# Expert numbers for TensorE: one load per routed job, or one load for four inside a gate_up group

## The chip, the cores and the metric

The kernel runs on one core of one Trainium2 chip. The metric is the device time of that core in microseconds (us), as the median of several runs. Three runs of the kernel before gave 379.7, 380.57 and 380.77 us.

## What is computed

The reference is one layer on 2048 tokens of 512 numbers: a cross attention and then a feed-forward part with experts. Cut to the second part, where the change lies:

```python
shared = silu(x @ shared_gate_w) * (x @ shared_up_w) @ shared_down_w
logits = x @ router_w                                  # 8 experts
top_val, top_idx = top_k(logits, 2)
probs[t, top_idx] = sigmoid(top_val)
xin = probs.T[:, :, None] * x[None]
gate, up = split(einsum('etd,edf->etf', xin, gate_up_w), 2)
out = x_in + shared + einsum('eti,eid->etd', silu(gate) * up, down_w).sum(0)
```

Here x is the layer-normed result of the attention part. D is 512, the inner width I is 256, and each token goes to two of the eight experts.

## The kernel before, in words

The work is written by hand as one instruction stream for each engine, tied together with semaphores. The first 16 tiles of 128 tokens run attention and, two tiles later, the shared expert as "jobs" 0 to 15. Then the router's choices are turned into tables. The token choices are sorted by expert and packed into 39 routed jobs of 128 rows, so `TILES` is 16, `ROUTED` 39 and `JOBS` 55. Each routed job has one expert, and its number (1 to 8) stands in the int32 tile `jexpert`, which VectorE writes once (L784). This text counts the routed jobs from 0 to 38.

Matmul operands are split in a high part (`x_hi`, `gu_hi`, `dn_hi`, 32-bit) and a low part. In one routed job the engines do this:

- GpSimd gathers 128 rows of normed x into `xg` by an indirect DMA (L406), four jobs ahead in a ring of four, and adds the result `y` to the output by an indirect DMA (L425). Both go through GpSimd's one queue, in the order gather of job n+4, scatter of job n. Ahead of a scatter the queue waits for `y` and for scatters of earlier jobs (for the first seven jobs: for all of the last three).
- TensorE transposes `xg` (`x_transpose`, L1021), multiplies by the expert's gate_up weights in `gate_up_high` (L909, four matmuls) and `gate_up_low` (L914 and L917, four each), transposes `h` (`h_transpose`, L926), and multiplies by the down weights in `down` (L936, L939, L942, two each).
- ScalarE computes `silu` from the finished gate_up bank (L574 loads the expert number, L575 is the activation), copies the transposed x to `x_hi` and `x_bf` (L490, L491) and the transposed h to `h_hi` and `h_bf` (L498, L499).
- VectorE computes h (L825 loads the expert number, L826), `x_lo` (L648), `h_lo` (L654) and the copy of y (L835).

TensorE's order in iteration n is fixed by the loop at the end of `_(pe)`: load the expert number of job n (L1028), wait for `x_hi` of job n (with others, L903 to L907), `gate_up_high(n)`, `h_transpose(n - 1)`, `gate_up_low(n)`, `x_transpose(n + 1)`, `down(n - 1)`. The four matmuls of L917 wait for `x_lo` of the job (L915), and the last one signals `g_ps`, on which ScalarE's `silu(n)` waits. The number `e` enters the addresses of the weights `gu_hi[:, e, k, :]` and so on, which TensorE's sequencer works out in small register instructions ahead of the matmuls.

[...] The first four jobs load a second number (`jlow`, L1030). The sequencer handles its instructions in order. [...]

Of the kernel before, what the change touches and what calls it, by code (L numbers as in the profile page):

```python
# [8 lines left out]
TILES = T // P  # L9
RT = S // P  # L10
KC = D // P
E, K, I = 8, 2, 256
# [3 lines left out]
ROUTED = (K * T + E * (P - 1)) // P  # L16
JOBS = TILES + ROUTED
# [17 lines left out]
def build(nc, x, ctx, mask, kpad, wq, bq, wk, bk, router_w, gate_up_w, down_w, sg_w, su_w, sd_w, out):  # L35
# [10 lines left out]
    with stack:  # L46
# [12 lines left out]
        def new(name, shape, dt=f32):  # L59
            offset = top_of[0]  # L60
            top_of[0] = (offset + int(np.prod(shape[1:])) * size[dt] + 31) // 32 * 32
            assert top_of[0] <= nc.sbuf_usable_end
            return at(offset, name, shape, dt)
# [81 lines left out]
        jexpert = new("jexpert", [P, ROUTED], i32)  # L145
# [47 lines left out]
        def ps_g(n):  # L193
            return bank[0] if n >= TILES and n % 2 else bank[4]
# [655 lines left out]
        def _(pe):  # L850
# [51 lines left out]
            def gate_up_high(n, e):  # L902
                pe.wait_ge(xhi_s, n + 1)  # L903
                if n > TILES + 1:
                    pe.wait_ge(h_s, n - 1)
                elif n:
                    pe.wait_ge(h_s, min(n, TILES))  # L907
                for k in range(KC):
                    tn.matmul(ps_g(n)[:], x_hi[:, n % TS, k, :], gu_hi[:, e, k, :], start=(k == 0), stop=False)  # L909

            def gate_up_low(n, e):
                pe.wait_ge(xbf_s, n + 1)
                for k in range(KC):
                    tn.matmul(ps_g(n)[:], x_bf[:, n % TS, k, :], gu_lo[:, e, k, :], start=False, stop=False)  # L914
                pe.wait_ge(xlo_s, n + 1)  # L915
                for k in range(KC):
                    last = tn.matmul(ps_g(n)[:], x_lo[:, n % TS, k, :], gu_hi[:, e, k, :], start=False, stop=(k == KC - 1))  # L917
                last.then_inc(g_ps, 1)

            def h_transpose(n):  # L920
                pe.wait_ge(h_s, n + 1)
                if n:
                    pe.wait_ge(hlo_s, n)
                    pe.wait_ge(hbf_s, n)
                for c in range(IC):
                    last = tn.transpose(ps_hT[:, c * P:(c + 1) * P], h[:, n % 2, c * P:(c + 1) * P], ident[:])  # L926
                last.then_inc(hT_ps, 1)

            def down(n, e):
                pe.wait_ge(hhi_s, n + 1)  # L930
                if n > TILES + 1:
                    pe.wait_ge(y_s, n - 1)
                elif n:
                    pe.wait_ge(y_s, min(n, TILES))
                for c in range(IC):
                    tn.matmul(ps_y(n)[:], h_hi[:, n % 2, c, :], dn_hi[:, e, c, :], start=(c == 0), stop=False)  # L936
                pe.wait_ge(hbf_s, n + 1)
                for c in range(IC):
                    tn.matmul(ps_y(n)[:], h_bf[:, n % 2, c, :], dn_lo[:, e, c, :], start=False, stop=False)  # L939
                pe.wait_ge(hlo_s, n + 1)  # L940
                for c in range(IC):
                    last = tn.matmul(ps_y(n)[:], h_lo[:, n % 2, c, :], dn_hi[:, e, c, :], start=False, stop=(c == IC - 1))  # L942
                last.then_inc(y_ps, 1)
# [28 lines left out]
            for s in range(TILES):  # L972
                j = s - LAG
                if s + 1 < B:
                    projections(s + 1)
                if s + 2 < B:
                    ctx_transpose(s + 2)
                if j == 0:
                    pe.wait_ge(lo_s, 3)
                if j >= 0:  # L980
                    gate_up_high(j, SHARED)
                    gate_up_low(j, SHARED)
                if j >= 1:
                    down(j - 1, SHARED)
                if s >= 1:
                    xn_transpose(s - 1)
                if s + 1 < TILES:
                    scores(s + 1)
                if j >= 0:
                    h_transpose(j)  # L990
                    logits(j)

            gate_up_high(TILES - 2, SHARED)
            gate_up_low(TILES - 2, SHARED)
            xn_transpose(TILES - 1)
            logits(TILES - 2)
            down(TILES - 3, SHARED)
            h_transpose(TILES - 2)
            logits(TILES - 1)
            gate_up_high(TILES - 1, SHARED)  # L1000
            gate_up_low(TILES - 1, SHARED)
            pe.wait_ge(pexp_s, TILES)
            ranks()
# [8 lines left out]
            def x_transpose(n):  # L1012
                pe.wait_ge(gt_xg[n % XS], 16 * ((n - TILES) // XS + 1))
                if n > TILES + 1:
                    pe.wait_ge(xbf_s, n - 1)
                    pe.wait_ge(xlo_s, n - 1)
                elif n == TILES:
                    pe.wait_ge(xbf_s, TILES)
                    pe.wait_ge(xlo_s, TILES)
                for k in range(KC):  # L1020
                    last = tn.transpose(ps_xT[n % 2][:, k * P:(k + 1) * P], xg[:, n % XS, k * P:(k + 1) * P], ident[:])  # L1021
                last.then_inc(xT_ps, 1)

            pe.wait_ge(expert_s, 1)
            x_transpose(TILES)
            before = None
            for n in range(TILES, JOBS):
                e = pe.value_load(jexpert[0:1, n - TILES:n - TILES + 1], min_val=0, max_val=E)  # L1028
                if n < TILES + XS:
                    low = pe.value_load(jlow[0:1, n - TILES:n - TILES + 1], min_val=6, max_val=CHUNKS)  # L1030
                    pe.wait_ge(lo_s, low)
                else:
                    pe.wait_ge(lo_s, CHUNKS)
                gate_up_high(n, e)
                if n > TILES:
                    h_transpose(n - 1)
                gate_up_low(n, e)
                if n + 1 < JOBS:
                    x_transpose(n + 1)
                if n > TILES:  # L1040
                    down(n - 1, before)
                before = e
# [24 lines left out]
```

## Time and profile before

| | |
|---|---|
| median of 3 runs | 380.57 us (379.7 to 380.77) |
| the profiled execution | 381.52 us |
| span of its trace | 379.8 us |
| mean granted TensorE clock in it | 0.945 of full speed |
| TensorE busy (matmul) | 331.9 us, 87% |
| VectorE, ScalarE, GpSimd busy | 209.4, 178.4 and 209.3 us |
| the routed jobs' first and last matmul group (L909) | 169.4 and 363.9 us |

Busy time counts matmuls and data instructions. The sequencer's own instructions (register work, loads of a register, waits) are not in it. They can be asked for by line, and then stand under a name that ends in q: PEldq is TensorE's sequencer, ACTq ScalarE's, DVEq VectorE's. [...]

### The profile page before, as it was taken

To read this page: it belongs to the slowest core of one execution; us is meant where nothing else is said; L and a number is where in the kernel's file an instruction comes from. 1 tells how busy PE (TensorE), PEld (TensorE's weight loads), DVE (VectorE), ACT (ScalarE), POOL (GpSimd) and SP (SyncE) were. 2 spreads that over 40 slices of the span, in tenths; PEclk is the share of its full clock that TensorE was granted. 3 is DMA by queue.
4 is the path that set the end of the run, shared out by engine and by line. 5 is a ranking of instruction groups with operands and counts; after the bars stand their busy time and mean duration, and the time that the engine had idled before them with its cause. 6 is when DMAs were issued, how large, how long until landed. Compare 5 with 4: busy or idle time off the path is not lost.

```text
span 379.8 us, 6456 instructions
## 1 busy us (share of the span) xinstructions
PE 331.9 (87%) x1601; PEld 218.8 (58%) x1627; DVE 209.4 (55%) x476; ACT 178.4 (47%) x401; POOL 209.3 (55%) x196
## 2 busy tenths in 40 slices
PE   2868999999999883258999999999999999999981
PEld 1335675667667552235666666666666666666650
DVE  1755888889988469951444334444343344444331
ACT  2467687577675433512443433344434433344430
POOL 0679999877756124075254465555555455555433
PEclk9978899999999898558999999999999999999997
DMA  7856687665563405150344566656655475665635
GB/s 191 301 177 221 183 270 235 211 212 205 176 214 110 168 4 172 25 169 6 78 76 94 83 118 115 135 98 113 103 106 103 99 117 108 113 112 90 108 40 73
DMA packets 29763, 50.61 MB, mean 133 GB/s; under 512 B 5472, under 2 KB 9312, under 8 KB 29728
## 3 DMA queue, kind: packets, MB, share of 16 engines
q0 software_dynamic: 9008, 21.66, 31.6%
q1 hardware_dynamic: 19232, 27.99, 23.1%
q10 hardware_dynamic: 1488, 0.54, 0.7%
q8 instruction: 16, 0.26, 0.3%
q14 instruction: 19, 0.16, 0.1%
HBM read 30.45 MB, written 19.73 MB: 132 GB/s over the span
## 4 chain that ended last, share of the span: by engine, by line
PE 46%; POOL 15%; issue 13%; DMA 8%; DVE 8%; ACT 7%; ACTq 1%; POOLq 0%; DVEq 0%
PE bank L909 11%; PE bank L917 8%; PE bank L914 8%; POOL gu_lo L348 5%; DMA out_rows<-y,jscatter 5%; PE bank L936 4%; PE bank L942 4%; PE bank L939 4%; PE bank L1021 4%; POOL rstd L325 3%; POOL dn_lo L348 3%; PE bank L926 2%; POOL pen L343 2%; ACT bank L472 2%; DMA kpad_in<-in_mask_BxS_bf 2%
## 5 line engine op out<-in xcount | busy, mean ns | idle before, releaser
L425 POOL DMA_INDIRECT out_rows<-y,jscatter x39 | 61.9, 1587 | 87.5 <-DMA out_rows<-y,jscatter 60.1
L826 DVE SCALAR_TENSOR_TENSOR h<-bank,xg,h 128x256 f32<-128x256 f32 x39 | 18.9, 484 | 106.1 <-ACT h L575 93.4
L917 PE MATMUL bank<-gu_hi,x_lo 128*128 (+1 forms) x220 | 71.5, 447 | 0.0
L909 PE MATMUL bank<-gu_hi,x_hi 128*128 (+1 forms) x220 | 67.4, 429 | 3.4 <-issue 3.1
L406 POOL DMA_INDIRECT xg<-xn_rows,jgather x39 | 41.5, 1063 | 29.0 <-DVE jgather L796 14.3
L914 PE MATMUL bank<-gu_lo,x_bf 128*128 (+1 forms) x200 | 55.7, 393 | 1.3 <-issue 0.2
L348 POOL TENSOR_TENSOR gu_lo<-stage,gu_hi 128x1024 bf16<-128x1024 f32 x18 | 42.6, 2372 | 23.6 <-ACT gu_hi L477 23.5
L575 ACT ACTIVATE h<-bank,xg 128x256 f32<-128x256 f32 x39 | 18.5, 474 | 74.5 <-PE bank L917 66.3
L909 PEld LDWEIGHTS bank<-gu_hi,x_hi 128*128 128x128 f32 x220 | 39.1, 193 | 24.9 <-issue 19.5
L917 PEld LDWEIGHTS bank<-gu_hi,x_lo 128*128 128x128 f32 x220 | 42.6, 194 | 13.4 <-issue 0.8
L942 PE MATMUL bank<-dn_hi,h_lo 128*128 (+1 forms) x110 | 46.0, 499 | 0.0
L498 ACT CAST h_hi<-bank 128x256 fp32r<-128x256 f32 x55 | 20.6, 374 | 51.9 <-PE bank L926 50.2
L648 DVE TENSOR_TENSOR x_lo<-bank,x_hi 128x512 fp32r<-128x512 f32 x55 | 37.3, 679 | 5.9 <-ACT x_bf L491 5.7
L936 PE MATMUL bank<-dn_hi,h_hi 128*128 (+1 forms) x110 | 38.9, 435 | 1.6 <-DVE x L668 1.0
L490 ACT CAST x_hi<-bank 128x512 fp32r<-128x512 f32 x55 | 32.0, 581 | 5.2 <-PE bank L1021 4.2
L939 PE MATMUL bank<-dn_lo,h_bf 128*128 (+1 forms) x104 | 32.7, 392 | 0.6 <-issue 0.2
L491 ACT CAST x_bf<-bank 128x512 bf16<-128x512 f32 x55 | 32.9, 598 | 0.0
L914 PEld LDWEIGHTS bank<-gu_lo,x_bf 128*128 128x128 bf16 x220 | 20.6, 100 | 19.7 <-issue 7.0
L654 DVE TENSOR_TENSOR h_lo<-bank,h_hi 128x256 fp32r<-128x256 f32 x55 | 23.1, 420 | 13.8 <-ACT h_bf L499 13.4
L926 PE MATMUL bank<-ident,h 128*128 128x128 f32 x110 | 21.8, 280 | 7.3 <-DVE h L662 6.2
L835 DVE COPY y<-bank 128x512 f32<-128x512 f32 x39 | 26.6, 682 | 1.1 <-PE bank L942 1.1
L926 PEld LDWEIGHTS bank<-ident,h 128*128 128x128 f32 x110 | 14.2, 141 | 22.6 <-DVE h L662 14.5
(125 smaller groups left out, 489.8 us busy)
## 6 DMA issues: line engine op xcount, KB each, us to landing
stage<-in_L_ffn_gate_up_w SPq DMA_DIRECT2D x16, 512.0 KB, 3.7
xin<-in_x SPq DMA_DIRECT2D x16, 256.0 KB, 4.5
xn_rows<-xn SPq DMA_DIRECT2D x16, 256.0 KB, 4.1
stage<-in_L_ffn_down_w SPq DMA_DIRECT2D x8, 512.0 KB, 3.9
out_rows<-x SPq DMA_DIRECT2D x16, 256.0 KB, 4.3
out_rows<-zeros POOLq DMA_DIRECT2D x1, 1024.0 KB, 5.0
ctx_in<-in_ctx SPq DMA_DIRECT2D x1, 768.0 KB, 8.7
xg<-xn_rows,jgather POOLq DMA_INDIRECT x39
```

Source lines behind the costliest of these rows:

```text
L348: g.tensor_tensor(third((gu_lo, dn_lo), c), stage[:, c % 3], third((gu_hi, dn_hi), c).bitcast(f32), ALU.subtract).then_inc(lo_s, 1)
L406: g.indirect_dma_start(out=xg[:, r, :], out_offset=None, in_=xn_dram, in_offset=bass.IndirectOffsetOnAxis(ap=jgather[:, n - TILES:n - TILE ...
L425: g.indirect_dma_start(out=out, out_offset=bass.IndirectOffsetOnAxis(ap=jscatter[:, n - TILES:n - TILES + 1], axis=0), in_=y[:, r, :], in_ ...
L491: a.copy(x_bf[:, n % TS], rows_T(n)).then_inc(xbf_s, 1)
L648: v.tensor_tensor(x_lo[:, n % TS], rows_T(n), x_hi[:, n % TS].bitcast(f32), ALU.subtract).then_inc(xlo_s, 1)
L909: tn.matmul(ps_g(n)[:], x_hi[:, n % TS, k, :], gu_hi[:, e, k, :], start=(k == 0), stop=False)
L914: tn.matmul(ps_g(n)[:], x_bf[:, n % TS, k, :], gu_lo[:, e, k, :], start=False, stop=False)
L917: last = tn.matmul(ps_g(n)[:], x_lo[:, n % TS, k, :], gu_hi[:, e, k, :], start=False, stop=(k == KC - 1))
L926: last = tn.transpose(ps_hT[:, c * P:(c + 1) * P], h[:, n % 2, c * P:(c + 1) * P], ident[:])
L936: tn.matmul(ps_y(n)[:], h_hi[:, n % 2, c, :], dn_hi[:, e, c, :], start=(c == 0), stop=False)
L939: tn.matmul(ps_y(n)[:], h_bf[:, n % 2, c, :], dn_lo[:, e, c, :], start=False, stop=False)
L942: last = tn.matmul(ps_y(n)[:], h_lo[:, n % 2, c, :], dn_hi[:, e, c, :], start=False, stop=(c == IC - 1))
```

## The change

One load for four jobs takes the place of a load at the head of each job. The first load (jobs 0 to 3) moves ahead of the transpose of the first routed job. The loads for jobs 4 to 7, 8 to 11 and so on up to 36 to 38 stand inside `gate_up_low` of jobs 3, 7, ..., 35, between the third and the fourth matmul of L917. Each load is one call over four neighbouring elements of `jexpert` (three in the last), with the same bounds for each value as before. Loads of `jlow` and the loads on ScalarE and VectorE stay.

```diff
+            experts = []
+
+            def load_experts(quad):
+                experts.extend(nc.values_load_multi_w_load_instructions(
+                    jexpert[0:1, 4 * quad:min(4 * quad + 4, ROUTED)], engines=[mybir.EngineType.PE], min_val=0, max_val=E)[1])
+
-            def gate_up_low(n, e):
+            def gate_up_low(n, e, quad=None):
...
                     last = tn.matmul(ps_g(n)[:], x_lo[:, n % TS, k, :], gu_hi[:, e, k, :], start=False, stop=(k == KC - 1))
+                    if k == 2 and quad is not None:
+                        load_experts(quad)
                 last.then_inc(g_ps, 1)
...
             pe.wait_ge(expert_s, 1)
+            load_experts(0)
             x_transpose(TILES)
             before = None
             for n in range(TILES, JOBS):
-                e = pe.value_load(jexpert[0:1, n - TILES:n - TILES + 1], min_val=0, max_val=E)
+                e = experts[n - TILES]
...
-                gate_up_low(n, e)
+                following = (n - TILES + 1) // 4
+                gate_up_low(n, e, following if (n - TILES) % 4 == 3 and n + 1 < JOBS else None)
```

## Rows read from the trace of the kernel before

**Rows 1.** The page: busy time by engine, and the granted clock in 40 slices.
```profile
PE 331.9 (87%) x1601; PEld 218.8 (58%) x1627; DVE 209.4 (55%) x476; ACT 178.4 (47%) x401; POOL 209.3 (55%) x196
...
PEclk9978899999999898558999999999999999999997
```

**Rows 2.** Timeline of TensorE's weight loads, two routed jobs: start, length, engine, line, operation, count.
```profile
248.19 0.76 PEld L909 LDWEIGHTS bank<-gu_hi,x_hi 128*128 128x128 f32 x4 [0.43 <-issue]
...
253.21 0.76 PEld L909 LDWEIGHTS bank<-gu_hi,x_hi 128*128 128x128 f32 x4 [0.43 <-issue]
```

**Rows 3.** Timeline of all engines, 250.8 to 253.6 us: from one job's gate_up to the next.
```profile
250.53 0.86 PE L917 MATMUL bank<-gu_hi,x_lo 128*128 x3
250.76 0.19 PEld L917 LDWEIGHTS bank<-gu_hi,x_lo 128*128 128x128 f32 x1
...
252.06 0.48 ACT L575 ACTIVATE h<-bank,xg 128x256 f32<-128x256 f32 x1 [1.78 <-PE bank L917]
...
252.43 0.58 ACT L490 CAST x_hi<-bank 128x512 fp32r<-128x512 f32 x1
```

**Rows 4.** L1028 and L905 on TensorE's sequencer, all jobs, then L905 in 250.5 to 253.6: min/median/max ns, first and last start.
```profile
L1028 PEldq TENSOR_LOAD <-jexpert x39: 296/302/948, 166.4 to 361.5; - x39
L1028 PEldq FUSED_REGOPS  x39: 151/151/165, 167.2 to 361.8; - x39
L1028 PEldq SEQ_ASSERT  x39: 18/18/32, 167.4 to 362.0; - x39
...
L905 PEldq EVENT_SEMAPHORE  x37: 393/1612/1884, 180.6 to 362.1; - x37
...
L905 PEldq EVENT_SEMAPHORE  x1: 1607/1607/1607, 251.4 to 251.4; - x1
```

**Rows 5.** Timeline of all engines, 253.1 to 256.7 us: the gate_up group of a job.
```profile
253.70 0.68 DVE L648 TENSOR_TENSOR x_lo<-bank,x_hi 128x512 fp32r<-128x512 f32 x1
...
256.01 0.59 PEld L1021 LDWEIGHTS bank<-ident,xg 128*128 128x128 f32 x4
...
256.57 0.30 PEld L936 LDWEIGHTS bank<-dn_hi,h_hi 128*128 128x128 f32 x2
```

**Rows 6.** L1016 (the wait behind L917) on TensorE's sequencer, 253.6 to 257 us.
```profile
L1016 PEldq EVENT_SEMAPHORE  x1: 51/51/51, 254.4 to 254.4; - x1
```

**Rows 7.** Timelines at 255.8 us (a weight load taken early) and 253.2 us (one that comes late).
```profile
255.55 0.85 PE L917 MATMUL bank<-gu_hi,x_lo 128*128 x3
255.78 0.19 PEld L917 LDWEIGHTS bank<-gu_hi,x_lo 128*128 128x128 f32 x1
...
253.21 0.19 PEld L909 LDWEIGHTS bank<-gu_hi,x_hi 128*128 128x128 f32 x1 [0.43 <-issue]
253.21 0.49 PE L909 MATMUL bank<-gu_hi,x_hi 128*128 x1
```

**Rows 8.** The same load and check on ScalarE's and VectorE's sequencers, all jobs.
```profile
L574 ACTq TENSOR_LOAD <-jexpert x39: 273/278/877, 174.7 to 367.1; - x39
L574 ACTq FUSED_REGOPS  x39: 152/152/167, 175.2 to 367.4; - x39
...
L825 DVEq TENSOR_LOAD <-jexpert x39: 299/303/876, 176.1 to 368.3; - x39
L825 DVEq FUSED_REGOPS  x39: 190/190/206, 176.7 to 368.6; - x39
```

**Rows 9.** Timeline of TensorE's weight loads, 216.9 to 228.6 us: routed jobs 9 to 11.
```profile
217.25 0.76 PEld L909 LDWEIGHTS bank<-gu_hi,x_hi 128*128 128x128 f32 x4 [0.45 <-issue]
...
220.63 0.42 PEld L1021 LDWEIGHTS bank<-ident,xg 128*128 128x128 f32 x4 [0.38 <-DMA xg<-xn_rows,jgather]
...
222.50 0.76 PEld L909 LDWEIGHTS bank<-gu_hi,x_hi 128*128 128x128 f32 x4 [0.27 <-issue]
...
226.29 0.42 PEld L1021 LDWEIGHTS bank<-ident,xg 128*128 128x128 f32 x4 [1.04 <-DMA xg<-xn_rows,jgather]
...
228.10 0.53 PEld L909 LDWEIGHTS bank<-gu_hi,x_hi 128*128 128x128 f32 x3 [0.21 <-issue]
```

**Rows 10.** The first routed job: L1018 and L1028 on the sequencer, and the timeline.
```profile
L1018 PEldq EVENT_SEMAPHORE  x1: 51/51/51, 165.1 to 165.1; - x1
...
L1028 PEldq TENSOR_LOAD <-jexpert x1: 697/697/697, 166.4 to 166.4; - x1
...
167.57 1.06 PE L1021 MATMUL bank<-ident,xg 128*128 128x128 f32 x4
```

## The prediction

> **What bounds the kernel now.** I read the page first: TensorE is busy for 87% of the span and its clock is granted in full through nearly all of the routed stage [rows 1]. That alone would say that TensorE's array is the limit and that work of its sequencer, which is in no busy figure, is free or nearly so. To see whether it is, I went to one job and laid four things side by side: the array, ScalarE, VectorE and TensorE's sequencer.
>
> The weight loads of L909 come every 5.02 us, 248.19 and 253.21 [rows 2]. What closes this loop is a chain through ScalarE. The last matmul of L917 ends at 250.53 + 0.86 = 251.39; ScalarE then loads its own expert number and starts silu at 252.06; `x_hi` is done at 252.43 + 0.58 = 253.01 [rows 3]; TensorE's sequencer, which has stood in the wait of L905 since 251.4, leaves it 1.607 us later, at about 253.05 [rows 4], and the first L909 weight load follows at 253.21 [rows 2]. From there to the end of L917 the array works without a gap that I can find. So the loop is: end of L917, ScalarE, `x_hi`, L909, L926, L914, L917. Anything that moves the end of L917 by a microsecond moves every later job by a microsecond, unless something else is waited for. The work between (L1021 and `down`) is beside that chain.
>
> The present load of L1028 lies in the free part. It costs the sequencer 0.302 + 0.151 + 0.018 us and three steps between instructions; from the last load's start at 361.5 to the wait behind it at 362.1 is about 0.65, so a step is 0.06 [rows 4]. The wait behind it then lasts 1.612 us in the median and 0.393 at least [rows 4]. The load is hidden with at least that to spare.
>
> **The change, part by part.** *Removed: 39 loads at the head of the jobs.* Worth 0, since the wait of L905 only begins 0.65 us earlier and ends with the same `x_hi`. What hides it is ScalarE's chain, and that stays. For the first job see below.
>
> *Added: nine loads inside L917, in jobs 3, 7, ..., 35.* Everything behind such a load on the sequencer is held up: the fourth matmul of L917 with the signal to ScalarE, then the waits, transposes and `down`. When does the sequencer get there, and when must the fourth matmul be out? It waits for `x_lo`, done at 253.70 + 0.68 = 254.38 [rows 5], and is already behind all of L917 at 254.4 (254.44 by the usual 0.06 step) [rows 6]. So the load starts at 254.44. The fourth matmul's weight load runs at 255.78 and its matmul ends at 255.55 + 0.85 = 256.40, 0.62 later; but a weight load that comes late is followed by a matmul that ends 0.50 after it, at 253.21 + 0.49 [rows 7]. So it may come as late as 255.90 and cost nothing. That gives a slack of 255.90 - 254.44 = 1.46 us.
>
> The checks of four values: each 0.151 + 0.018 and two steps of 0.06, 0.285 as the rows add up with unrounded steps of 0.058; four make 1.14. I take one check per value, as now. With the step behind the load that is 1.20, and 0.26 us of slack remain for the load itself.
>
> The load of four has no row. Its bounds are 0.30 (one read whatever the number, one row of L1028) and 4 x 0.302 = 1.21 (four reads in a row). To place it between them I compare engines: the same register work takes 0.152 on ScalarE and 0.190 on VectorE, 1.25 times as much, but the same load takes 0.278 and 0.303, only 1.09 times [rows 8]. If 1.25 is the ratio of the sequencers, the load is about 0.10 us of sequencer work and about 0.18 of a wait that does not scale; for TensorE's 0.302 the wait is then about 0.20. I take it that the 0.10 is paid once and the wait once per number: 0.302 + 3 x 0.20 = 0.90. That the wait is paid per number is the weak step of my sum. [...]
>
> The delay of such a job is then 0.90 + 1.20 - 1.46 = 0.64 us. At the lower bound it is 0.04, at the upper 0.95. The last load has three values: one read and one check less, so 0.64 - 0.20 - 0.285 = 0.15 (0 and 0.35 at the bounds). What stands behind the load besides L917 has more room: L1021's weight loads run at 256.01 and those of `down` at 256.57 [rows 5], and the delayed loop moves them along. ScalarE, VectorE and GpSimd all wait for TensorE and are shifted, not slowed.
>
> *Absorbed.* Jobs 10 and 11 start 222.50 - 217.25 = 5.25 and 228.10 - 222.50 = 5.60 after their forerunners, because their transposes wait for gathers [rows 9], which hang on GpSimd's chain of scatters, each waiting for the one before. These 0.23 + 0.58 = 0.81 us are wait that a TensorE arriving late no longer has. The delays of jobs 3 and 7 come before it, 1.28 us together, so 0.81 is given back.
>
> *Moved: the first load.* The sequencer is at the wait of L1018 at 165.1, and the first load took 0.697 there (I take the extra as a cold start); the transposes run at 167.57, behind `down` [rows 10]. The new load starts at about 165.1 and takes 0.70 + 0.60 + 1.20, then about 0.1 for the waits: the transposes are handed out at 167.7 at the earliest, and at the half clock of this stretch begin perhaps 0.2 later. That is 0.3 us late, 0 at the lower bound and 0.6 at the upper.
>
> **Sum**: 0.3 + 2 x 0.64 - 0.81 + 6 x 0.64 + 0.15 = 4.8 us, where the six are jobs 11 to 31. The profiled execution took 381.52 us and would take 386.3; it stood 0.95 above the median of 380.57, and so the forecast for the median is 385.3. At the lower bound: the first two delays are absorbed, 6 x 0.04 = 0.2. At the upper: 0.6 + 1.9 - 0.81 + 5.7 + 0.35 = 7.7.
>
> **The rivals.** *B, the load of four costs about what one costs.* Then the delay is 0.04 in each of six jobs: 380.8 us, no change. For it: it is one instruction, and four neighbouring numbers are 16 bytes. Against it: the rows of ScalarE and VectorE, which put most of a load into a wait of fixed length, and which say nothing on whether four such waits overlap. It holds as long as the load stays under about 0.45 us, since 6 x (0.45 - 0.26) is 1.1 us.
>
> *C, faster: TensorE's load disturbs ScalarE's.* ScalarE's load of L574 is on the loop. It begins when L917 ends, at 251.39 [rows 3], which is about when TensorE's own load and check are over and the wait of L905 begins [rows 4]. If the neighbour lengthens it, 38 jobs get shorter. For the change to be faster by over 0.3% it would have to be 0.03 us per job; at 0.05 it is 380.57 - 1.9 + 0.2 = 378.9 us, with a cheap load. Against it: the loads do not overlap, and ScalarE's shortest is 0.273 against a median of 0.278 [rows 8], which offers 38 x 0.005 = 0.2 us.
>
> *D, the call doesn't do what it says* and issues four loads. Then a job pays 4 x 0.647 = 2.59 on the sequencer, 1.13 more than the slack: 0.7 + 2.26 - 0.81 + 6.8 + 0.5 = 9.4, 390.0 us. The words of the change speak against it; if the numbers are read each by itself, it is nearly the upper bound.
>
> **How the numbers follow.** A measurement of this kernel can tell about 0.3%, 1.1 us, from no change. I give the forecast 0.58, B 0.32, C 0.04 and D 0.06. The forecast's own range is 383.5 (a load of 0.70: 0.1 + 0.88 - 0.81 + 6 x 0.44, 2.8 in all) to 388.3 us. The range takes in B's 380.8 with a little of the runs' spread and the upper bound of the load: 380.3 to 388.5, which leaves out C and D. Slower by over 0.3%: forecast and D, less a small part of the forecast with a load near 0.45, 0.63. Within 0.3%: 0.33. Faster: 0.04.
>
> **What would show it.** In the changed profile: ten TENSOR_LOAD rows for TensorE at the helper's line, nine of about 0.9 us (B: 0.3) and 39 checks of 0.151; the weight loads of L909 in the jobs behind such a load (12, 16, ..., 32) 5.66 us after the forerunner's instead of 5.02, and in the others still 5.02; the fourth weight load of L917 late, with an idle stretch on the array in front of it that is put down to issue; the gather waits ahead of jobs 10 and 11 gone; L905 waiting about 2.2 us in the other jobs. The prediction is wrong if the load of four takes under 0.45, if the checks are fewer than one per value, if the sequencer reaches the third matmul of L917 at another time than 254.44, or if the jobs without a load get shorter too, which none of my steps allows.

## The result, and the profile after

The changed kernel takes 382.54 us (median of 18 runs, 380.98 to 384.0), the kernel before 380.83 us in 18 runs beside it. The ratio is 1.0042, with a 95% interval of 1.0027 to 1.0058. So the change makes the kernel slower, by 1.6 us where 4.8 had been forecast. (Executions in a slow state are left out of the ratios, here and below, so a ratio need not equal the quotient of the medians.) The sign and the place were right, and the size was three times too large. The profiled execution took 383.6 us, with a span of 381.8, against 381.52 and 379.8 before.

The page shows nothing of it. These are its engine line and its clock, to be read beside [rows 1]:

```profile
PE 332.2 (87%) x1601; PEld 217.8 (57%) x1627; DVE 209.3 (55%) x476; ACT 178.6 (47%) x401; POOL 209.6 (55%) x196
...
PEclk9989899999999898558999999999999999999998
```

TensorE is as busy as before (332.2 us against 331.9), and its clock was granted alike (0.952 of full speed in the mean against 0.945). The load itself is the first thing to look up. The helper's line on TensorE's sequencer, all jobs, answers to [rows 4]:

```profile
L914 PEldq FUSED_REGOPS  x39: 146/151/165, 165.8 to 352.8; - x39
L914 PEldq SEQ_ASSERT  x39: 18/18/27, 166.0 to 353.0; - x39
L914 PEldq TENSOR_LOAD <-jexpert x10: 328/333/1037, 165.2 to 351.1; - x10
```

There are ten loads and 39 checks, one for each value, as expected. (The kernel that leaves the comparison with the bounds out, below, has the ten TENSOR_LOAD rows on this line and none of the other two kinds, so FUSED_REGOPS and SEQ_ASSERT, 0.151 and 0.018 us, are the check.) The sequencer also reaches the loads when it was expected to, 1.23 us after the first L909 weight load of the job (270.34 against 269.11; 254.44 against 253.21 in the prediction). But a load of four takes 0.333 us, 0.03 more than a load of one, where I had put 0.90. Is the fourth matmul late all the same? The timeline of TensorE's weight loads over one job with a load of four in it (L923 is the L917 of before, L1029 the L1021):

```profile
269.11 0.76 PEld L909 LDWEIGHTS bank<-gu_hi,x_hi 128*128 128x128 f32 x4 [0.44 <-issue]
...
271.01 0.64 PEld L923 LDWEIGHTS bank<-gu_hi,x_lo 128*128 128x128 f32 x3
271.92 0.19 PEld L923 LDWEIGHTS bank<-gu_hi,x_lo 128*128 128x128 f32 x1 [0.27 <-issue]
272.05 0.57 PEld L1029 LDWEIGHTS bank<-ident,xg 128*128 128x128 f32 x4
...
274.23 0.41 PEld L909 LDWEIGHTS bank<-gu_hi,x_hi 128*128 128x128 f32 x2 [0.43 <-issue]
```

It is. Three weight loads of L923 come in one piece. The fourth stands alone behind 0.27 us of idle "issue": the sequencer is at the load and its checks from 270.34 to 271.87, this weight load follows 0.05 later, and the wait behind it (L1024) begins at 271.95, one after the other in the order of the program. The next job starts 5.12 us after this one, where a job without a load needs 5.02 [rows 2]. The eight starts behind the loads in jobs 3 to 31 come after 5.37, 5.21, 5.21, 5.12, 5.12, 5.12, 5.11 and 5.15 us; the first of them took 5.30 before the change as well. In the waits of the weight loads over the routed stage this is a new line:

```profile
PEld bank L923 <- issue: 2.7, 8, 0.6
```

Eight such waits, 2.7 us in all, the longest 0.6. Of the usual 0.27 about 0.10 reaches the loop: 0.04 lies between two such loads in any job, and a late weight load gives back 0.12, since its matmul ends 0.50 us behind it instead of 0.62 [rows 7].

The longest one is the last. In job 35 the load took 1.037 us instead of 0.333, and the next job started 5.77 us later (355.69 - 349.92), where the kernel before needed 5.30. These rows are the load, GpSimd's gather ahead of it, and the two starts, each from its own view:

```profile
L914 PEldq TENSOR_LOAD <-jexpert x1: 1037/1037/1037, 351.1 to 351.1; - x1
```

```profile
350.30 1.06 POOL L406 DMA_INDIRECT xg<-xn_rows,jgather  x1 [0.30 <-issue]
```

```profile
349.92 0.76 PEld L909 LDWEIGHTS bank<-gu_hi,x_hi 128*128 128x128 f32 x4 [0.44 <-issue]
355.69 0.77 PEld L909 LDWEIGHTS bank<-gu_hi,x_hi 128*128 128x128 f32 x4 [0.72 <-issue]
```

This last load is the only one that asks for three numbers instead of four, and the rows say that this by itself makes it slow. In the kernel with the loads at the head of the jobs (below), where it stands 2.7 us behind the start of a gather, it takes 0.772 us, and the load of four before it, at nearly the same distance, 0.333:

```profile
L914 PEldq TENSOR_LOAD <-jexpert x1: 333/333/333, 326.9 to 326.9; - x1
...
L914 PEldq TENSOR_LOAD <-jexpert x1: 772/772/772, 347.1 to 347.1; - x1
```

In all eight kernels with loads of four the load of three takes 0.77 to 1.33 us. In the kernel before, the single loads at 346 and 351 us take 0.30, so the place in the program is not enough to explain it. What comes on top goes with the gather ahead of it (last section): in the seven kernels with the old line on ScalarE the load of three starts 0.84, 0.89, 0.92, 1.01, 1.09, 1.14 and 2.68 us behind the start of a gather and takes 1.037, 0.981, 0.955, 0.862, 0.783, 0.777 and 0.772. It was not tried in another job.

**The account of the two traces.** From the first L909 weight load of job 0 to that of job 38 it is 194.44 us before and 196.28 after, 1.84 more. The eight jobs behind the loads in jobs 3 to 31 hold 0.94 of this (41.42 against 40.48 us). The job behind the slow last load holds 0.47. Jobs 9 to 11 hold 0.12, and 0.3 is spread over jobs 1, 5, 37 and others. Besides, job 0 starts 0.09 us later (169.54 against 169.45), but the transposes ahead of it, and `down` ahead of these, are late by the same 0.09, so this is not the moved load.

### The profile page after: what moved, and what is told of

It reads as the page before. It is cut to its first block, busy times and chain, and to the rows that moved or that the text cites. A ratio compares the mean times of both kernels' runs of the same rounds, so it can differ in the third digit from the quotient of the medians.

```text
span 381.8 us, 6426 instructions
## 1 busy us (share of the span) xinstructions
PE 332.2 (87%) x1601; PEld 217.8 (57%) x1627; DVE 209.3 (55%) x476; ACT 178.6 (47%) x401; POOL 209.6 (55%) x196
## 4 chain that ended last, share of the span: by engine, by line
PE 60%; POOL 13%; issue 10%; ACT 8%; DVE 7%; DMA 1%; SPq 0%; DVEq 0%; ACTq 0%; POOLq 0%
PE bank L909 13%; PE bank L923 11%; PE bank L920 10%; PE bank L944 5%; PE bank L950 5%; POOL gu_lo L348 5%; PE bank L947 5%; PE bank L1029 5%; PE bank L934 3%; POOL dn_lo L348 3%; POOL rstd L325 2%; ACT gu_hi L477 2%; ACT bank L472 2%; DMA ctx_in<-in_ctx 1%; PE bank L868 1%
## 5 line engine op out<-in xcount | busy, mean ns | idle before, releaser
L923 PE MATMUL bank<-gu_hi,x_lo 128*128 (+1 forms) x220 | 73.3, 454 | 0.2 <-issue 0.2
L909 PE MATMUL bank<-gu_hi,x_hi 128*128 (+1 forms) x220 | 66.9, 427 | 5.6 <-issue 4.0
L909 PEld LDWEIGHTS bank<-gu_hi,x_hi 128*128 128x128 f32 x220 | 38.6, 191 | 27.3 <-issue 20.8
L923 PEld LDWEIGHTS bank<-gu_hi,x_lo 128*128 128x128 f32 x220 | 43.0, 195 | 16.1 <-issue 3.7
```

## The experiments

Ratios are to the kernel before, in runs on the same chip. Single runs of these kernels scatter by up to 1.6% on some chips (376.4 to 382.43 us for the kernel before), so beside each ratio I give a stretch of the trace that is free of the early jobs: from the start of job 12 to that of job 35. It takes 115.42 us before and 116.06 in the changed kernel. Five of the starts in it come behind a load of four. Each stretch is from one trace; the two kernels at the end that add loads on SyncE and leave TensorE's stream as before give 115.42 and 115.52, so 0.1 us is noise. The "slot" is the place of the loads of four, between the third and the fourth matmul of L917 (L923), and the "slot theory" of the expectations is that a load there costs only what it delays this fourth matmul.

**The loads behind the group.**

```diff
-                    if k == 2 and quad is not None:
+                    if k == 3 and quad is not None:
                         load_experts(quad)
```

> The nine loads stand behind the fourth matmul of L917 instead of in front of it; all else is as in the changed kernel. Slot theory (the cost is that the fourth matmul, and with it the signal to ScalarE, is held up by 0.10 us behind load and checks): the fourth matmul is no longer late, the jobs behind a load take 5.02 us like all others, and the time is within 0.1% of before (ratio 0.999 to 1.001). Rival, whatever the load holds up on the sequencer counts (transposes, down, waits): the ratio stays at about 1.004. Rival, the cost is the new place of the first load or the registers: 1.004 as well.

Measured: ratio 1.0003 (0.9974 to 1.0033), stretch 115.83 us. The four weight loads of L923 come in one piece again, and it is L1029 that now waits, with no effect on the loop:

```profile
270.30 0.86 PEld L923 LDWEIGHTS bank<-gu_hi,x_lo 128*128 128x128 f32 x4
271.38 0.43 PEld L1029 LDWEIGHTS bank<-ident,xg 128*128 128x128 f32 x4 [0.21 <-issue]
...
273.43 0.77 PEld L909 LDWEIGHTS bank<-gu_hi,x_hi 128*128 128x128 f32 x4 [0.43 <-issue]
```

The jobs behind the loads take 5.01 to 5.04 us. So of all that the load holds up, the fourth matmul with its signal is what counts. The interval just excludes the rival's 1.004; the rows say it more clearly. But jobs 17, 21, ..., 33, one further on, now take 5.06 to 5.11, and the stretch is still 0.4 us above before. This part the slot theory does not explain. In the sequencer's records the step between the end of the L905 wait and the next register instruction is 0.10 to 0.15 us at the starts of these jobs and 0.055 elsewhere. Such steps come up again below.

**No bounds checks.**

```diff
-                    ..., engines=[mybir.EngineType.PE], min_val=0, max_val=E)[1])
+                    ..., engines=[mybir.EngineType.PE], min_val=0, max_val=E,
+                    skip_runtime_bounds_check_because="jexpert is clamped to 1..E where it is written")[1])
```

> The loads stand where the change puts them, but without the comparison with the bounds, so that four values cost the sequencer one load of 0.33 us and no checks. Slot theory: 0.4 us instead of 1.58, which is a microsecond less than the slack, so the fourth matmul is on time and the ratio is 0.999 to 1.001. Rival, the read itself disturbs TensorE or the others wherever it stands in the group: the jobs behind a load stay 0.1 us longer and the ratio stays near 1.004.

Measured: ratio 1.0018 (0.9989 to 1.0046), stretch 115.93. This kernel leaves out the comparison of each number with its bounds. The load takes 0.333 as before, and the group is whole:

```profile
267.19 0.77 PEld L909 LDWEIGHTS bank<-gu_hi,x_hi 128*128 128x128 f32 x4 [0.43 <-issue]
...
269.10 0.87 PEld L924 LDWEIGHTS bank<-gu_hi,x_lo 128*128 128x128 f32 x4
272.22 0.76 PEld L909 LDWEIGHTS bank<-gu_hi,x_hi 128*128 128x128 f32 x4 [0.44 <-issue]
```

Here a load of four stands in the job at 267.19, and the next starts 5.03 later. The read as such cost nothing; the four checks that follow it, 1.14 us of the 1.58, are what fills the slack. Two of the starts behind a load, those of jobs 24 and 32, come after 5.17 and 5.18, though. Their groups are whole too; what differs is a step of 0.21 us instead of 0.055 between the end of the L905 wait and the first register instruction of L909. These two make 0.3 of the 0.5 us by which the stretch is above before. The interval of the ratio excludes neither expectation; the rows decide.

**One more load.**

```diff
                         load_experts(quad)
+                        pe.value_load(jexpert[0:1, 0:1], min_val=0, max_val=E)
```

> Behind each of the nine loads one more single load with its check, whose value is not used, in the same place. It adds 0.65 us on the sequencer. Slot theory: there is no slack left in that place, so the jobs behind a load grow from 5.12 to 5.77 us each, and the kernel by 7 x 0.65 = 4.6 us (the loads ahead of job 10 are partly taken up by the wait for gathers) up to 9 x 0.65 = 5.9 over the changed one: a ratio of 1.016 to 1.020. Rival, the 0.10 us per load have another cause and the slack is larger than I think: below 1.010.

Measured: ratio 1.0155 (1.0105 to 1.0206), stretch 119.86. The wait of the fourth weight load grows to 0.80:

```profile
271.09 0.19 PEld L923 LDWEIGHTS bank<-gu_hi,x_lo 128*128 128x128 f32 x1 [0.80 <-issue]
...
273.41 0.76 PEld L909 LDWEIGHTS bank<-gu_hi,x_hi 128*128 128x128 f32 x4 [0.44 <-issue]
```

The ratio is just below what I had expected (1.016 to 1.020), and its interval reaches over it. The jobs behind a load take 5.70 to 5.74 us in the steady stretch, 0.6 more than with one load less. This is the slack, measured: it was used up already, and 0.65 us more of the sequencer in this place came back as 0.6 us of the loop. Jobs 21, 25, 29 and 33, one further on, also grew, to 5.17 to 5.33; VectorE's own load took 0.8 to 0.96 us instead of 0.30 there. More on that below.

**The slot two matmuls earlier.**

```diff
-                    if k == 2 and quad is not None:
+                    if k == 0 and quad is not None:
```

> The changed kernel with the loads of four between the first and the second matmul of L917 instead of between the third and the fourth. The sequencer gets there at the same time, but the matmul behind the load is due 0.46 us earlier (two matmuls of 0.23). Slot theory: the jobs behind a load grow from 5.12 to 5.58 us, 7 to 9 times 0.46 more than the changed kernel, 3.2 to 4.1 us, ratio 1.012 to 1.016. Rival, the place inside the group doesn't matter, only the time on the sequencer: 1.004.

Measured: ratio 1.0132 (1.0104 to 1.016). The rows show the wait at the second weight load, and job starts 5.57 us apart:

```profile
268.76 0.77 PEld L909 LDWEIGHTS bank<-gu_hi,x_hi 128*128 128x128 f32 x4 [0.43 <-issue]
...
271.56 0.53 PEld L923 LDWEIGHTS bank<-gu_hi,x_lo 128*128 128x128 f32 x3 [0.70 <-issue]
...
274.33 0.76 PEld L909 LDWEIGHTS bank<-gu_hi,x_hi 128*128 128x128 f32 x4 [0.43 <-issue]
```

5.57 is 5.12 + 0.46, within a hundredth. The same work on the sequencer, begun at the same time, costs 0.45 us more where its matmul is due 0.46 sooner. Jobs 21, 25, 29 and 33 grew here as well, to 5.28 to 5.34, again with a VectorE load of 0.92 to 0.97 us. The four kernels so far, and the next one, fit one sum within 0.05 us in their usual jobs: delay = sequencer work minus the time until the held matmul is due (0.70 us for work of 2.23, 0.55 with the slot two matmuls earlier, and none in the other three).

**A single load in every group.**

```diff
-                experts.extend(nc.values_load_multi_w_load_instructions(...
+                experts.append(pe.value_load(jexpert[0:1, job:job + 1], min_val=0, max_val=E))
...
-                gate_up_low(n, e, following if (n - TILES) % 4 == 3 and n + 1 < JOBS else None)
+                gate_up_low(n, e, n - TILES + 1 if n + 1 < JOBS else None)
```

The load for job 0 stands behind the transpose of the first routed job here.

> A single load with its check (0.65 us on the sequencer) between the third and the fourth matmul of L917 in every job, for the next job; no load of four. It tests the slack of 1.46 us from below. Slot theory: 0.65 is hidden in every job, ratio 0.999 to 1.002. Rival, a load inside the group breaks the queue of matmuls whatever it takes: 38 times 0.1 us, a ratio near 1.010.

Measured: ratio 1.0023 (0.9981 to 1.0066), stretch 115.51, 0.09 above before, which is noise. All 23 periods in the stretch are 5.00 to 5.05 us. A load with its check is 0.65 us and within the slack of 1.48. So in this group one check at a time costs nothing, and four in a row, 1.58 us with their load, cost 0.10.

**The loads of four at the old place.**

```diff
-            load_experts(0)
             x_transpose(TILES)
...
+                if (n - TILES) % 4 == 0:
+                    load_experts((n - TILES) // 4)
                 e = experts[n - TILES]
...
-                gate_up_low(n, e, following if (n - TILES) % 4 == 3 and n + 1 < JOBS else None)
+                gate_up_low(n, e)
```

> The loads of four with their checks, but at the head of jobs 0, 4, 8, ..., where the single loads stood. Slot theory: load and checks take about 1.5 us there and the wait for x_hi behind them lasts 2.2 us without a load, so they are hidden, no job is longer than 5.03 us in the steady stretch, and the ratio is 0.999 to 1.001. Rival, loads of four or their registers cost something wherever they stand: 1.003 or more.

Measured: ratio 1.0036 (0.9998 to 1.0075) by the runs, medians 381.25 and 380.94; stretch 115.73. The jobs with a load in front take 5.02 to 5.04, as expected. Jobs 21, 25, ..., 33 take 5.06 to 5.07. The ratio alone would speak for the rival, though its interval takes in 1.000; the stretch shows 0.3 us. I leave it at that: there is a small cost of 0.1 to 0.5 us in every version with loads of four that does not come from the slot.

**The first load back in its place.**

```diff
-            load_experts(0)
             x_transpose(TILES)
+            load_experts(0)
```

> Only the first load is put back behind the transpose of the first routed job; the nine others stay inside L917. Slot theory: this gives back at most the 0.24 us by which the first routed job starts later, ratio 1.003 to 1.004. Rival, the first load is most of the cost: ratio below 1.002.

Measured: ratio 1.0055 (1.0026 to 1.0085), stretch 116.42. Nothing is gained, so the first load is not the cost. The 0.24 us of the expectation is not in the rows: the transposes of the first routed job start 1.21 or 1.22 us behind the start of `down`'s last line in the kernel before, in the changed one (167.66 - 166.45) and in the one with the load put back, so the moved load delays nothing. The kernel is, if anything, slower: in two jobs of the stretch the fourth weight load waits 0.36 us and the next job comes after 5.22. A step inside the first of the four checks was 0.21 there instead of 0.06, in the same instructions. The last load, of three numbers, takes 0.783 here, and the start behind it comes after 5.54: 0.24 us more than before the change, where 1.037 cost 0.47.

**Eight numbers in a load.** The loads stand at the head of jobs 0, 8, 16, ..., and none is in the slot; this kernel leaves the comparison with the bounds out.

```diff
+                if (n - TILES) % 8 == 0:
+                    load_experts((n - TILES) // 8)
```

> Loads of eight numbers without bounds checks, at the head of jobs 0, 8, 16, .... It prices a load by its size. If the size adds about 0.01 us per number, as between one (0.302) and four (0.333), a load of eight takes 0.37 us; if what is fetched at once is 16 bytes, it takes about 0.36 plus another read of up to 0.2, so 0.5 to 0.6.

Measured, the load on TensorE's sequencer from 245 to 295 us:

```profile
L914 PEldq TENSOR_LOAD <-jexpert x2: 588/590/593, 249.4 to 289.7; - x2
```

One number takes 0.302, four 0.333, eight 0.59. These two are the loads of eight that stand far from a gather; the two earlier ones took 0.871 and 1.326, 0.86 and 0.14 us behind the start of one. The last load of this kernel asks for seven numbers, 2.5 us behind the start of a gather:

```profile
L914 PEldq TENSOR_LOAD <-jexpert x1: 1068/1068/1068, 329.9 to 329.9; - x1
```

So the sizes stand at 0.302 (1), 0.77 (3), 0.333 (4), 1.07 (7) and 0.59 (8). They would fit one read for four numbers where four are left, and a read for each single number where fewer are: about 0.24 us for each further read, an estimate from (0.772 - 0.302) / 2 and (1.068 - 0.333) / 3, and 0.26 from four to eight. That is argued from the sizes that happened to occur; the rows show whole loads and no single read, and 2, 5 and 6 numbers were not tried. The one timed run gave 381.39 us.

**ScalarE's load ahead of its waits, in both kernels.**

```diff
             def silu(n):
+                e = act.value_load(jexpert[0:1, n - TILES:n - TILES + 1], min_val=1, max_val=E)
                 act.wait_ge(g_ps, n + 1)
                 act.wait_ge(hT_ps, n - 1)
-                e = act.value_load(jexpert[0:1, n - TILES:n - TILES + 1], min_val=1, max_val=E)
```

> The kernel before, with one line moved on ScalarE: the load of the expert number (L574) stands ahead of the waits for g_ps and hT_ps instead of behind them. If the loop is closed through ScalarE as I read it, load and check (0.53 us) leave the loop, and the period of a job falls from 5.02 us until TensorE's array has no gap left: of the 0.53 only about 0.27 us can be had, a period near 4.75, some 10 us over 38 jobs, a ratio of 0.972 to 0.980. Rival, TensorE's array is the limit already: ratio 1.00.

Measured: 369.79 us, ratio 0.9748 (0.9667 to 0.9829). The timeline of the weight loads:

```profile
251.65 0.89 PEld L909 LDWEIGHTS bank<-gu_hi,x_hi 128*128 128x128 f32 x4
...
255.96 0.41 PEld L942 LDWEIGHTS bank<-dn_hi,h_lo 128*128 128x128 f32 x2
256.40 0.65 PEld L909 LDWEIGHTS bank<-gu_hi,x_hi 128*128 128x128 f32 x3
```

The period is 4.75 us, the idle "issue" in front of L909 [rows 2] is gone, and the weight loads of one job follow those of the last without a gap (256.37 to 256.40): I read this as the array being the limit now. This confirms the reading of the loop on which the prediction stood, and it is the version that beats both kernels.

> The same line moved in the changed kernel. The loop is shorter, x_low comes as early as before relative to the start of a job, and the slack of the slot stays, so the nine loads should cost the same 0.1 us or somewhat more each: a ratio to before of 0.975 to 0.985, 0.003 to 0.005 above the kernel before with the same line moved. Rival, with TensorE's array as the limit the loads no longer cost anything: the two are alike.

Measured: 371.81 us, ratio 0.98 (0.9719 to 0.9881), 2 us above the kernel before with the same line moved. The ratio lies inside what I had expected, but by luck: my reason, 0.1 us per load, missed. The group with a load in it is whole, and the period 4.75:

```profile
279.87 0.89 PEld L909 LDWEIGHTS bank<-gu_hi,x_hi 128*128 128x128 f32 x4
...
281.90 0.87 PEld L923 LDWEIGHTS bank<-gu_hi,x_lo 128*128 128x128 f32 x4
284.62 0.89 PEld L909 LDWEIGHTS bank<-gu_hi,x_hi 128*128 128x128 f32 x4
```

The fourth weight load of L923 runs 1.62 us behind the start of the load of four here (282.58 against 280.96), where in the kernel before it ran 1.34 behind the time that the slot is reached (255.78 against 254.44), and the 1.58 us fit. What is left is in single jobs: 0.27 us behind a load of 0.76 and 0.58 behind the load of three, 1.33 here, both begun 0.5 to 0.7 us behind the start of a gather, and in jobs 9 and 10 0.30 and 0.57 more than in the kernel before with the line moved.

**Loads on an idle engine.** The slow loads called for a probe. In the kernel before, SyncE loads and drops numbers in jobs 12 to 31.

> The kernel before, with twelve single unchecked loads in a row on SyncE's otherwise idle sequencer in each of the routed jobs 12 to 31. It samples what a load costs at each time after GpSimd's gather (L406) begins. Theory from the slow loads of all traces so far: loads that start within about 1 us behind the start of a gather take 0.5 to 1.0 us, all others 0.30. Rival, the slow loads have another cause (a given place in the instruction streams): no relation to the gather. The time should stay within 0.3% of before unless the loads disturb each other.

The trace has no rows for these loads, so this run (381.7 us, one run) says nothing about them. The question was put again with checks, six in a row per job:

```diff
+            for n in range(TILES + 12, TILES + 32):
+                sp.wait_ge(g_ps, n + 1)
+                for i in range(6):
+                    sp.value_load(jexpert[0:1, 0:1], min_val=0, max_val=E)
```

> The unchecked loads on SyncE of the last run left no rows in the trace, so the question is put again with checks: the kernel before, with six single loads and checks in a row on SyncE in each of the routed jobs 12 to 31. Theory: loads that start within about 1 us behind the start of a gather (L406) take 0.5 to 1.0 us, all others 0.30. Rival: no relation to the gather. Time within 0.3% of before.

Measured: 380.87 us in one run, with 379.08 in one of the kernel before beside it, and 120 loads. One gather of GpSimd (L410 here), and the two loads on SyncE that began 0.6 and 1.7 us after it:

```profile
247.14 1.06 POOL L410 DMA_INDIRECT xg<-xn_rows,jgather  x1 [0.30 <-issue]
```

```profile
L303 SPq TENSOR_LOAD <-jexpert x1: 812/812/812, 247.7 to 247.7; - x1
...
L303 SPq TENSOR_LOAD <-jexpert x1: 267/267/267, 248.8 to 248.8; - x1
```

All 20 loads that began 0.2 to 0.8 us after the start of a gather took 0.59 to 0.96 us. Of the 98 that began at least 1.2 us after one, the longest took 0.462, two more 0.41 and 0.37, and all others under 0.28.

## Why the prediction was right or wrong

**What bounds the kernel: right.** The loop closed through ScalarE and `x_hi` and not by the array. Shortening ScalarE's part gave the 4.75 us per job that was expected from the 0.27 us gap.

**The removed loads are worth nothing: right.** Jobs without a load of four kept 5.02 us. The wait of L905 grew from 1.612 to 2.256 us in the median, 0.64 us, which is what the load and its check had taken.

**The slack of 1.46 us: right within 0.02 us.** Load, checks and steps took 1.58 us and cost 0.10, which makes the slack 1.48. TensorE's sequencer was as far ahead of the array as I had read: in the kernel before it is at the wait of L1016, behind L917, at 254.44, and the first weight load of L917 runs at 255.10, the fourth at 255.78. Both the extra load (0.65 us more work, 0.6 more delay) and the earlier slot (due 0.46 sooner, 0.45 more) moved the delay as the difference of work and due time says. This is the part of the mechanism that the experiments show.

**The load of four at 0.90 us: wrong, and this is the step that failed.** It takes 0.333. I had split the price of one load into work of the sequencer and a wait of 0.20, and had called it the weak step that the wait is paid per number. The split was my estimate, and no run shows it. What the runs show is 0.333 for four numbers and 0.59 for eight. Only the loads of three and of seven, 0.772 and 1.068, are as dear as if each number past the last whole four were paid by itself, at about 0.24 us each further one (the estimate above). With 0.333 in the sum the delay is 0.07 per job instead of 0.64, and the six jobs that stand for 3.84 us in the sum cost 0.7 together. Rival B was right on the price of the load.

**Why it was still not "no change", as rival B had it:** three things that B had not counted.

- The last step of the four checks is 0.12 us in four of the eight slots of jobs 3 to 31, 0.21 in two and 0.09 in two, not 0.06, which lifts the delay to 0.10 and more.
- The last load. The sum has it one read and one check cheaper than the others, 0.15 us. One check fewer is right, but the load of three is dearer than a load of four, not cheaper. It takes 0.772 us and more against 0.333, 1.037 in this trace and 0.77 to 0.98 in the traces of the other kernels with ten loads of four and the old line on ScalarE. It costs 0.47 us here, the half of it by the size (0.24 at 0.783 us, with the first load back in its place), the other half by being slower still behind a gather.
- 0.1 to 0.5 us come from small steps of TensorE's sequencer that recur about every four jobs. They are in the kernel before too: nine steps of 0.21 to 0.23 us between 185 and 350 us, there inside L909 and L936, where the jobs still take 5.02. The changed programs shift them, into the checks or between the L905 wait and L909, where they reach the loop. In the trace's DMA records a transfer of 16 KB of the kind "instruction" follows each of the nine within 1.0 to 2.4 us. Whether the steps come from this was not tested, so their cause stays open.

**The 0.81 us given back at jobs 10 and 11: wrong in its cause.** I had read the gather waits of L1021 [rows 9] as the cause of the two long jobs. But L1021 is beside the loop, as my own first part says. What made the jobs long were register loads on the loop's path: 0.876 us on VectorE at 216.6 (0.57 more than usual, of which 0.23 reach the next start) and 0.877 on ScalarE at 225.7 (0.60 more, and the next start is 0.58 late), each behind the start of a gather. In the kernel before:

```profile
L825 DVEq TENSOR_LOAD <-jexpert x1: 876/876/876, 216.6 to 216.6; - x1
...
L574 ACTq TENSOR_LOAD <-jexpert x1: 877/877/877, 225.7 to 225.7; - x1
```

In the changed kernel TensorE waits for no gather there, and jobs 9 and 10 are 0.37 and 0.57 us long beyond 5.02, for ScalarE's loads of these jobs took 0.38 and 0.57 more than 0.278:

```profile
L574 ACTq TENSOR_LOAD <-jexpert x1: 662/662/662, 215.9 to 215.9; - x1
...
L574 ACTq TENSOR_LOAD <-jexpert x1: 847/847/847, 221.3 to 221.3; - x1
```

So nothing was given back here: jobs 9 to 11 together take 0.12 us more than before. But behind a delay as large as the 1.28 us that I had put ahead of them it may be. With one more load, and with the slot two matmuls earlier, jobs 4 and 8 together are late by 1.55 and 1.15 us, no load on ScalarE or VectorE meets a gather in jobs 9 to 11, and these three take 15.05 and 15.10 us, 0.83 and 0.79 less than the 15.88 of before. So the size would have come out right with a large delay, by another way than the one that I gave: the shift moves register loads out of the way of the gathers. This is one trace each, and the two kernels with loads on SyncE, whose TensorE works as before, have 15.39 and 16.24 in these jobs, so the 0.8 us is not priced well, and the 0.12 lies within this scatter.

**The first load's move: 0.3 us forecast, nothing measured.** The load took 0.522 us where 1.30 stood in the sum (that the 0.697 of the kernel before had a cold start in it was my guess, and no run shows it), and the transposes came out no later behind `down` than before. Putting it back did not show in the time either.

**Rival C** (TensorE's load disturbs ScalarE's) found no support: without a neighbour ScalarE's load still takes 0.273 us at least and 0.278 in the median.

**A slip in the working:** the lower end of the forecast's own range should read 383.4 us (380.57 + 2.8), not 383.5.

## What to carry to other kernels

In this kernel TensorE's sequencer ran ahead of the array, by 0.66 us at the first weight load of L917 (254.44 against 255.10), and work on it was free only up to the time at which the next matmul was due: of a slack of 1.48 us, 0.65 cost nothing, 1.58 cost 0.10 and 2.23 cost 0.70. Find that time before placing a load, and count the bounds checks, which here cost more (1.14 us) than the load that they guard (0.33). If numbers are loaded in a batch, look at its size: here three took more than twice as long as four (0.772 against 0.333), and reading a fourth that nobody needs might have saved part of the 0.47 us of the last load (argued from the rows, not run). Batching the scalar loads gained nothing here, where each was hidden (the jobs without one kept 5.02 us); look instead for the one that stands behind the semaphore which closes the loop. Moving that line on ScalarE ahead of its wait was worth 2.5%.

## What the runs showed of the hardware that was not expected

- A register load of four neighbouring int32 numbers took 0.03 us more than one of a single number (0.333 against 0.302), and one of eight 0.29 more. One of three took 0.47 more (0.772 at the least, in eight traces), and one of seven 0.77 more (1.068, once).
- The register loads that started 0.2 to 0.8 us after GpSimd began an indirect gather took 0.6 to 1.3 us instead of 0.3, on TensorE, VectorE, ScalarE and SyncE alike. In eleven of the fourteen traces (without the kernel with loads of eight and the two with loads on SyncE), from 180 us on, 35 of 35 such loads took over 0.45 us, and in the probe 20 of 20 on SyncE. Of the 1980 loads in the same eleven traces that started at least 1.2 us after a gather's start, 13 took over 0.45: twelve of GpSimd's own at about 0.50, and the load of three at 0.772. In between, from 0.8 to 1.2 us, 13 of 44 did, six of them the load of three. Around 165 to 168 us it did not hold: in six of all fourteen traces a load of `jlow` began 0.4 to 0.6 us behind a gather and took 0.31 to 0.32. Why loads behind a gather took longer was not tried.
